# A six-layer decoder on one core: the first layer's "agents" stage with all 32 batches as rows of one PSUM bank

## The reference, cut to what matters

```python
def _L0_attn_ref(x, w_qkv, w_conv1):            # x: (32, 100, 256)
    qkv = jnp.einsum('bnc,dc->bnd', x, w_qkv)
    q, k, v = ...                               # 256 columns each
    agent = jnp.einsum('bnc,c->bn', q, w_conv1)
    agent_attn = softmax(jnp.einsum('bn,bnc->bc', agent * c ** -0.5, k), axis=-1)
    agent_v = softmax(jnp.einsum('bc,bnc->bn', agent_attn, v), axis=-1)
    agent_v = jnp.einsum('bn,bnc->bc', agent_v, v)
    agent_tok = softmax(agent[:, :, None], axis=-1)
    return agent_tok * agent_v[:, None, :]

x = _layernorm(x + _L0_attn_ref(x, ...))
x = _layernorm(x + _L0_xattn_ref(x, ctx, ctx, cell_mask, seq_mask, ...))   # scores + log(cell) + log(seq)
x = _layernorm(x + _L0_ffn_ref(x, ...))         # top 50 of 100 tokens, 16 heads
x = _layernorm(x + _L1_attn_ref(x, ...))        # 16 heads, banded
x = _layernorm(x + _L1_xattn_ref(x, ctx, ctx, ...))
x = _layernorm(x + _L1_ffn_ref(x, ...))         # int8 weights
```

## Time and profile before

| | |
|---|---|
| median of three runs | 1002.06 us |
| the profiled execution | 997.09 us, of which the span from first to last instruction 995.3 us |
| PE busy | 856.5 us, 86% |
| DVE, ACT, POOL busy | 640.5, 510.9, 374.7 us |
| TensorE's mean granted clock | 0.919 of full |
| DMA | 54.11 MB, mean 54 GB/s |
| chain that ended last | PE 56%, DVE 18%, ACT 13%, DMA 4%, POOL 4% |

### The profile page before, as it was taken

One profiled execution on the slowest core, in us unless ns is written; L12 is line 12 of the kernel. 1 busy time (PEld: TensorE's weight loads), 2 busy tenths in 40 slices (PEclk: granted clock), 3 DMA queues, 4 the chain that ended last, 5 costly groups with the idle time before them and its releaser, 6 DMA issues.

```text
span 995.3 us, 19801 instructions
## 1 busy us (share of the span) xinstructions
PE 856.5 (86%) x7054; PEld 642.7 (65%) x7054; DVE 640.5 (64%) x2064; ACT 510.9 (51%) x2392; POOL 374.7 (38%) x528
## 2 busy tenths in 40 slices
PE   7867899989896899997989879899989788989783
PEld 5745777756575777664667758676667666766462
DVE  4224766565878666666687873748665876576546
ACT  3103346887532546864655244776745444666541
POOL 0045502444655132245344430437452542234233
PEclk9766999999798999997999989989979979999697
DMA  7921400001243000012032300003211020000000
GB/s 229 282 62 64 170 1 2 2 17 30 102 159 107 21 10 2 2 40 86 9 102 88 102 18 1 18 8 111 79 33 71 9 97 1 2 2 1 1 9 26
DMA packets 23384, 54.11 MB, mean 54 GB/s; under 512 B 3697, under 2 KB 9589, under 8 KB 23285
## 3 DMA queue, kind: packets, MB, share of 16 engines
q1 hardware_dynamic: 23284, 52.84, 16.3%
HBM read 49.53 MB, written 3.31 MB: 53 GB/s over the span
## 4 chain that ended last, share of the span: by engine, by line
PE 56%; DVE 18%; ACT 13%; DMA 4%; POOL 4%; issue 3%; SPq 1%; DVEq 0%; POOLq 0%; ACTq 0%
PE psum L416 10%; PE psum L421 9%; ACT work L764 7%; PE psum L455 7%; PE psum L441 6%; PE psum L579 4%; PE psum L590 3%; DVE bn L879 2%; ACT work L729 2%; PE psum L600 2%; DVE x L887 2%; PE psum L582 2%; PE psum L411 2%; PE psum L497 1%; PE psum L514 1%
## 5 line engine op out<-in xcount | busy, mean ns | idle before, releaser
L764 ACT ACTIVATE work<-psum,mx 100x100 f32<-100x100 f32 x512 | 169.7, 370 | 52.3 <-DVE mx L1039 52.0
L764 ACT ACTIVATION_READ_ACCUMULATOR work<-psum,mx 100x1 f32 x512 | 119.5, 234 | 0.0
L658 ACT ACTIVATE xT<-psum 128x100 f32<-128x100 f32 (+3 forms) x144 | 52.9, 377 | 112.4 <-PE psum L411 48.1
L1125 POOL TENSOR_SCALAR ve<-mv 100x2 f32<-100x2 f32 x96 | 21.6, 225 | 227.7 <-DVE mv L882 227.2
L455 PE MATMUL psum<-eT,ctx 128*128 128x100 f32 x768 | 97.7, 282 | 0.5 <-DVE eT L916 0.4
L455 PEld LDWEIGHTS psum<-eT,ctx 128*128 128x128 f32 x768 | 94.3, 199 | 2.6 <-issue 0.7
L1154 POOL COPY work<-rden 100x128 f32<-100x128 f32 (+1 forms) x80 | 25.2, 317 | 180.2 <-DVE rden L1043 149.5
L441 PE MATMUL psum<-ctxT,qT 128*100 128x361 f32 x256 | 88.8, 492 | 4.8 <-ACT qT L677 3.9
L658 ACT ACTIVATE eT<-psum 100x400 f32<-100x400 f32 (+3 forms) x128 | 64.3, 517 | 39.5 <-PE psum L618 24.2
L590 PE MATMUL psum<-ident,work 100*100 100x100 f32 x512 | 69.1, 263 | 17.1 <-ACT work L764 16.7
L887 DVE TENSOR_SCALAR x<-res,mv,rstd 100x256 f32<-100x256 f32 x160 | 67.7, 465 | 24.4 <-POOL rstd L1127 24.0
(11 more groups left out here) (228 smaller groups left out, 2005.6 us busy)
## 6 DMA issues: line engine op xcount, KB each, us to landing
ctx<-in_ctx SPq DMA_DIRECT2D x16, 768.0 KB, 7.5
ctxT<-in_ctxT SPq DMA_DIRECT2D x16, 722.0 KB, 5.0
cell<-in_cell SPq DMA_DIRECT2D x16, 282.0 KB
seq<-in_seq SPq DMA_DIRECT2D x16, 282.0 KB
x<-in_x SPq DMA_DIRECT2D x16, 200.0 KB
eT<-agent_rows SPq DMA_DIRECT2D x16, 200.0 KB
out<-xplus SPq DMA_DIRECT2D x16, 200.0 KB
work<-in_x SPq DMA_DIRECT2D x4, 400.0 KB
```

The lines of the kernel that those rows point to most:

```text
L658: return e.activation(dst, src, ACT.Copy, **kw)
L764: last = e.activation(s.e[:, h, :], bk[g][0:S, q * S:(q + 1) * S], ACT.Exp, bias=s.mx[0:S, h:h + 1], accum_out=s.den[0:S, h:h + 1])
```

## The change

The agents' stage keeps its mathematics and changes its form:

- The weights of a batch are now eight columns, of which only the column of its slot is not zero. All 32 batches are accumulated into one bank: batch j of slot i is row 32j + i. DVE writes ag straight into that zeroed room (`token_w` in D's `qT`; `key_w` in A's and B's), and three matmuls with zeros open the banks.
- The first sums are made slot by slot among the transposes. One copy of 256 columns and two transposes take the place of four copies and 16 matmuls, twice. The softmax of the logits is one instruction, its sum is a small matmul, and the division is done on the agent's vector.
- The products of weights change places: `spread` for `wqbk` and the small `bqbk` come behind the logits; `wqk` and `wvo` leave the stage and are made at the start of streams C and D.
- For the first turn a stream does not load its agents from DRAM: two matmuls with a one-hot column spread the rows of `agent_v` (now a tile of its own) over 100 partitions in PSUM, and DVE reads them there.
- The masks of the first turn have rooms of their own in each stream (`v` and `kT`): all four pairs are loaded and multiplied on POOL during the agents' stage; the two DVE instructions, the logarithm and the sum follow in the stream's first turn. `vs` and `v` are cleared there too, stream by stream.
- SP's order: `w8` and `wscale` join `ld_c`; then the four pairs of masks, x, four loads that the second layer needs (`ld_first`), the contexts of A and B, the rest (`ld_const`, now waited for ahead of the pick stage), and the contexts of C and D.
- `ORDER` has new tables for all five engines.

```diff
+        key_w = [s.qT[:, :, :].rearrange("p c t -> p (c t)")[:, 0:SLOTS * B] for s in (SA, SB_)]
...
+        def own_columns(part):
+
+            return bass.AP(tensor=part.tensor, offset=part.offset, ap=[part.ap[0], (ROWS * SLOTS + 1, SLOTS), (SLOTS, ROWS)])
...
-            def rows_to_columns():
+            def weighed(bank, i, weights):
+
+                for j in range(ROWS):
+                    b = ROWS * i + j
+                    last = e.matmul(psum[32 * j:32 * j + SLOTS, bank, 0:D], weights[:, b * SLOTS:(b + 1) * SLOTS], x_of(b),
+                                    start=False, stop=i == SLOTS - 1, skip_group_check=True)
+                return last
+
+            def columns_of_rows():
                 for c in range(NC):
-                    for i in range(SLOTS):
-                        at_ = (c * SLOTS + i) * ROWS
-                        last = e.matmul(psum[:, 7, at_:at_ + ROWS], y_rooms[i // 2][:, i % 2, c * P:(c + 1) * P],
-                                        ident[:, 0:P:32], start=True, stop=True)
+                    last = e.transpose(psum[:, 7, D + c * P:D + (c + 1) * P], yrow[:, c * P:(c + 1) * P], ident[:, :])
                 return last
...
-            for i in range(SLOTS):
-                e.wait_ge(*agent_dve(f"ag{i}"))
-                for j in range(ROWS):
-                    b = ROWS * i + j
-                    last = e.matmul(psum[32 * j:32 * j + 32, i // 2, i % 2 * D:(i % 2 + 1) * D],
-                                    ag[:, b:b + 1].to_broadcast([S, 32]), x_of(b), start=True, stop=True)
-                last.then_inc(*agent_pe.up(f"y{i}"))
-            e.wait_ge(*agent_act("row1"))
-            e.wait_ge(*agent_dve("row1"))
-            rows_to_columns().then_inc(*agent_pe.up("yT1"))
+                if i:
+                    e.wait_ge(*agent_dve(f"ag{i - 1}"))
+                    weighed(7, i - 1, token_w)
+            e.wait_ge(*agent_dve("ag7"))
+            weighed(7, SLOTS - 1, token_w).then_inc(*agent_pe.up("y"))
...
+            e.wait_ge(*agent_act("x15"))
             spread(4, cols["a_bv"], W["a_o"]).then_inc(*agent_pe.up("p0"))
-            spread(5, cols["c_bk"], W["c_qT"]).then_inc(*agent_pe.up("p1"))
+            spread(5, cols["c_bv"], W["c_o"]).then_inc(*agent_pe.up("p2"))
...
-                        last = e.matmul(psum[32 * j:32 * j + 32, i // 4, i % 4 * P:i % 4 * P + S],
-                                        zT[:, c, b:b + 1].to_broadcast([P, 32]), xT_of(c, b),
-                                        start=c == 0, stop=c == NC - 1)
+                        last = e.matmul(psum[32 * j:32 * j + SLOTS, 0, 0:S], key_w[c][:, b * SLOTS:(b + 1) * SLOTS], xT_of(c, b),
+                                        start=False, stop=i == SLOTS - 1 and c == NC - 1, skip_group_check=True)
             last.then_inc(*agent_pe.up("log"))
-            e.wait_ge(*agent_dve("p3"))
+            e.wait_ge(*agent_dve("p0"))
+            spread(4, cols["c_bk"], W["c_qT"]).then_inc(*agent_pe.up("p1"))
+            e.wait_ge(*agent_dve("p2"))
+            for c in range(NC):
+                last = e.matmul(psum[:, 5, 0:1], cols["c_bk"][:, c:c + 1].to_broadcast([P, P]), cols["c_bq"][:, c:c + 1],
+                                start=c == 0, stop=c == NC - 1)
+            last.then_inc(*agent_pe.up("p3"))
+            e.wait_ge(*agent_act("lexp"))
+            e.transpose(psum[0:S, 7, 0:P], lrow, ident[:, :]).then_inc(*agent_pe.up("col"))
+            e.wait_ge(*agent_dve("acol"))
+            for i in range(SLOTS):
+                last = weighed(1, i, token_w)
+            last.then_inc(*agent_pe.up("u"))
+            e.wait_ge(*agent_dve("acol2"))
+            e.matmul(psum[0:B, 6, D:D + 1], acol, ones[0:S, 0:1], start=True, stop=True).then_inc(*agent_pe.up("sum"))
+            e.wait_ge(*agent_dve("p1"))
             for h in range(NC):
...
-                    last = e.matmul(psum[:, 5, h * D:(h + 1) * D], W["c_qT"][:, c, h * P:(h + 1) * P], W["c_kT"][:, c, :],
-                                    start=c == 0, stop=c == NC - 1)
...
-            last.then_inc(*agent_pe.up("p6"))
-            e.wait_ge(*agent_dve("ln"))
-            for i in range(SLOTS):
-                last = e.matmul(psum[0:S, 7, i * ROWS:(i + 1) * ROWS], l_rooms[i // 4][:, i % 4, :], ident[:, 0:P:32],
-                                start=True, stop=True)
...
-                last.then_inc(*agent_pe.up(f"u{i}"))
-            e.wait_ge(*agent_act("row2"))
-            e.wait_ge(*agent_dve("row2"))
-            rows_to_columns().then_inc(*agent_pe.up("yT2"))
+            e.wait_ge(*agent_dve("yr2"))
+            columns_of_rows().then_inc(*agent_pe.up("yT2"))
             e.wait_ge(*agent_dve("yT2"))
             for c in range(NC):
...
+            def weights(w, v):
+                for h in range(NC):
+                    last = columns(bk[1][:, h * D:(h + 1) * D], w, h, lambda c: v[:, c, :])
+                last.then_inc(*s.tensor["start"].up("weights"))
+
             for t in range(TURNS):
+                if t == 0:
+
+                    e.wait_ge(*agent_dve("v"))
+                    if s is SC_:
+                        weights(W["c_qT"], W["c_kT"])
+                    elif s is SD:
+                        weights(W["c_vT"], W["c_o"])
+                    for b in range(NB):
+                        n = NB * s.pair(t) + b
+                        last = e.matmul(bk[0][0:S, b * D:(b + 1) * D], ident[0:B, n:n + 1].to_broadcast([B, S]), agent_v[:, :],
+                                        start=True, stop=True)
+                    last.then_inc(*s.tensor["start"].up("rows"))
+                    yield
                 yield from cross(t, "first", s.vector["mix"], W["x_k"], W["x_o"])
 
...
+            e.memset(token_w, 0.0)
+            for part in key_w:
+                last = e.memset(part, 0.0)
+            last.then_inc(*agent_dve.up("zero"))
...
+                if t == 0 and s in (SC_, SD):
+                    e.wait_ge(*s.tensor["start"]("weights"))
+                    e.tensor_scalar((wqk if s is SC_ else wvo)[:, :, :].rearrange("p c n -> p (c n)"), bk[1],
+                                    INV if s is SC_ else 1.0, None, ALU.mult).then_inc(*s.vector["start"].up("weights"))
                     yield
 
                 pe, act, dve, pool = s.at("mix")
                 e.wait_ge(*s.load_x(t))
-                e.wait_ge(*s.load_agent(t))
+                if t:
+                    e.wait_ge(*s.load_agent(t - 1))
+                else:
+                    e.wait_ge(*s.tensor["start"]("rows"))
                 for b in range(NB):
                     if t:
                         e.wait_ge(*s.vector["quant"](f"x{b}", t - 1))
                     n = NB * s.pair(t) + b
-                    e.scalar_tensor_tensor(s.res[0:S, b, :], s.agent[:, b, :], tok[:, n:n + 1], s.x[0:S, b, :],
-                                           ALU.mult, ALU.add).then_inc(*dve.up(f"r{b}"))
+                    e.scalar_tensor_tensor(s.res[0:S, b, :], s.agent[:, b, :] if t else bk[0][0:S, b * D:(b + 1) * D],
+                                           tok[:, n:n + 1], s.x[0:S, b, :], ALU.mult, ALU.add).then_inc(*dve.up(f"r{b}"))
                 stats(dve, t)
                 yield
...
-
-            e.wait_ge(*agent_pe("u7"))
+            for s in streams:
+                masks_product(e, s, 0)
+
+            e.wait_ge(*SD.gpsimd["mask"]("prod", 0))
+            e.wait_ge(*agent_pe("u"))
             for s in streams:
                 last = e.memset(s.work[32 * (ROWS - 1):P, 0:H * HALF], 0.0)
             last.then_inc(*agent_pool.up("rows"))
-            e.wait_ge(*agent_pool("rows"))
-            e.wait_ge(*agent_dve("w8"))
-            e.wait_ge(*agent_pe("yT2"))
-            for s in streams:
-                e.memset(s.v_pick[:, :, :, :], 0.0)
-                last = e.memset(s.v[:, :, :, :], 0.0)
-            last.then_inc(*agent_pool.up("zeros"))
+            e.wait_ge(ld_first, LD_FIRST)
 
         def gpsimd_turns(e, s):
...
+            def zeros():
+
+                e.wait_ge(*agent_dve("v"))
+                e.wait_ge(*s.gpsimd["mask"]("sum", 0))
+                e.memset(s.v_pick[:, :, :, :], 0.0)
+                e.memset(s.v[:, :, :, :], 0.0).then_inc(*s.gpsimd["start"].up("zeros"))
...
+                if t == 0:
+                    masks_sum(e, s, t)
+                    zeros()
+                    yield
...
-            load_masks(e, SA, 0)
...
-            for n in WEIGHTS:
-                if n not in EARLY and n != "a_o":
-                    weight(n, ld_const)
...
-            e.dma_start(slots[:, :, :], ins["slots"]).then_inc(ld_const, 16)
-            load_ctx(e, SA, 0)
-            load_ctx(e, SB_, 0)
+            e.dma_start(w8_i, ins["w8"].rearrange("(c p) n -> p c n", p=P)).then_inc(ld_c, 16)
+            e.dma_start(wscale[:, :], ins["wscale"].to_broadcast([P, 1])).then_inc(ld_c, 16)
+            for s in streams:
+                load_masks(e, s, 0)
```

(23 more changed lines are left out.)

335 lines of the change are left out of this document (156 added, 179 removed).

## The result

The changed kernel took 1009.15 us (median), the kernel before, beside it on the same chip, 1004.75 us. The ratio is 1.006, with a 95% interval of 1.0039 to 1.0081. The forecast was 982 us.

The account below looks back on a forecast made before the run. PE was taken as the bound, behind a serial agents' stage and a thin ramp. Stage 16.3 plus ramp 4.1, loop nothing, gave 20.4 us off 1002.06: about 982 us, 8 in 10 range 966 to 1000.

Parts of the forecast that it names:

- Link 1: Agents' stage, start of the spread products: at 31.1 instead of 33.77 us, a gain of 2.7 (bounds nothing to 6).
- Links 3 and 5: Agents' stage, logits (4.56 us) and second sums (5.39): nothing gained, within 1 us and minus 2.5 to plus 2.
- Links 2, 4 and 6: Agents' stage, spread products to logits, logits to second sums, sums to vector: gains of 2.7, 5.8 and 5.1 us.
- The ramp: Start of the streams, from the agent's vector to 125 us: 51.4 us instead of 55.5, a gain of 4.1.
- For the loop I take nothing, plus or minus 8 us: Main loop: same instructions, only the order tables new, so no change taken, plus or minus 8 us (1%).
- The slower rival: Loop: streams run too close together and load DVE, 30 us lost against 20 gained, total 1012 us; chance 0.12.
- POOL holding the ramp: Start of the streams: POOL's work delays DVE and streams C and D, ramp gives back 8, 990 us; chance 0.17.
- the end gaining: End of the kernel, 925 to 950 us: three streams fill PE, 9 us come back, 973 or less; chance 0.15.
- The stage that doesn't shorten: Agents' stage: late loads and a lower clock put the vector at 60 us, total 990 to 998; chance 0.08.

Follow-up runs that it names:

- after: The changed kernel itself, with its own new order tables throughout, against the kernel before: 1009.15 us (median), ratio 1.006.
- experiment 3: Changed kernel with its new order only for PE's first 104 steps, the old order for the rest: 986.05 us, ratio 0.9818 to the kernel before.
- experiment 2: Kernel before, with its own order for PE's first 146 steps and the new tables' order for the rest: 1035.99 us, ratio 1.0317.
- the spliced kernel: Same kernel as experiment 3: changed code, new order to PE's step 104, old order behind it: 986.05 us.

## Why the prediction was wrong

- **Link 1** (spread products at 31.1): 30.89, right by luck. I had the last load of `ld_c` decide, and the key product done near 27 or 28. The load had landed at 29.0, and PE went to the spread products straight from the key product, which began at 29.05 and took 1.92, because the first sums ended only at 27.5. (My own terms, 31.85 less 2.2 plus 1.0, also give 30.65 and not 31.1.)
- **Links 3 and 5** (logits and second sums as long as before): too careful. They took 2.8 for 4.56, beyond my bound of 1 us, and 3.5 for 5.39. The granted clock is 1.00 all through to 64 us; before, it was 0.62 in the logits and 0.68 in the second sums, and 4.56 x 0.62 = 2.8, 5.39 x 0.68 = 3.7. I had read durations at a partly lower level as if they were the instructions' own. That is 3.6 us of the 5 by which the vector came earlier than my 53.2.
- **Links 2, 4 and 6** (forecast to last 5.4, 2.6 and 4.2): 5.7, 2.0 and 3.3. Right, to within a microsecond each.
- **The ramp**: a gain of 4.1 forecast. Behind the vector it is 3.7 (25 us of head, 21.3 of them in the stage). D's first transposes came at 74.55, forecast near 75. Right, though the 3 us that I added for a lower clock at its start weren't there (1.00 to 64 us, 0.84 from 64 to 75).
- **"For the loop I take nothing, plus or minus 8 us"** is the step that failed: it put the cost of the new tables at nothing, although the rows could not tell how they fit. The part from 125 us on (100 in after) is 36.5 us longer, and the mark that I had set (PE's share in the loop within 1% of 0.89 at 0.94) came out as 0.85 at 0.91. The order behind the head costs 23 us with one code (experiment 3 against after); in the old code it costs 31 us, seam included (experiment 2). The rest of the 36.5 us is 11 us of PE's busy time, spent on equal instructions, and 3 us of idle time, which the spliced kernel has as well against the profiled execution of before. That execution lay 8 us under the median of its kernel, so this part is partly the spread of the runs; how much isn't settled.
- **The slower rival** had nearly the right time, 1012, and the right place for the worst stretch, an end of turns where three streams run close. It had the wrong price: it let DVE's amount of work starve PE. With 49 us less on DVE the distance to the old order stayed (20.8 us). The mark I had set for it, DVE over 21 and PE under 18 of 25 us, shows once in the loop (775 to 800 us: 22.46 and 17.79); in the worst stretch DVE has only 19.26, for it stands too. What the traces show there is engines that stand in their order at a step that isn't ready, in part for loads that come in one bunch. I gave this rival 0.12. What could have weighed it, each engine's step beside the load or chain that feeds it, I didn't read.
- **POOL holding the ramp** and **the end gaining**: POOL's lock was there (a normalization of 2.59 us at 54.71 and one of 2.64 at 70.90, as 2.12 in the earlier trace rows), but PE had work. The rule of the Trainium skill (SBUF — State Buffer, "Who interferes with whom") that GpSimd and a DVE instruction in a two-port mode lock each other out of a shared pair of ports agrees with these rows. The masks' share of the lock doesn't make the loss in the loop, since cutting them helped the old order as much (1.5%) as the new (1.3%). The end did run better (21.21 us of PE at 0.93 from 925 to 950 us, for 19.51 at 0.59), on top of a loop that had already lost more.
- **The stage that doesn't shorten**: refuted by the first fence.

## What to carry to other kernels

A table of steps is an edit of the whole loop, however small the change beside it: cost it first, by putting the old order into the new code and the new order into the old code, and keep the new one only for the stretch that gains by it. Place the seam with care and try several: seams at steps 60 to 125 lay within 5 us of one another, one at 410 cost 49 us more than the one at 104. To gain from an order, go down the list of the longest waits of the bounding engine, follow each back through the in-order engines to a load, and check on the sync engine's own queue which step it stood at; one swap there was worth 0.5 to 0.8% here, while the swap beside it was worth nothing. Removing a suspect alone (loads, or work) can leave a distance untouched, 22.5 and 20.8 of 23 us here, where removing both left 12.3; take both away before either is acquitted, and run often enough to tell such numbers apart.

## What the runs showed of the hardware

- The logits' 64 matmuls of 100 columns (128 records) took 4.56 us before, at a granted clock of 0.62, the lower level for part of them, and 2.8 us after, at 1.00 throughout: 1.6 times less, as much as the clock gives, though their weights had shrunk from 32 columns to 8. What brought the clock down before isn't shown: from 27.5 us to the logits PE was busy 12.38 of 14.30 us before, and 7.55 of 9.13 after.
- Small DVE instructions between tiles of SBUF were stretched beside POOL's mask products: the scaling of 32x256 elements took 1.58 us from 32.22 and a product of 100x32 elements 1.58 us from 37.51, and each ended within 0.15 us of POOL's product (31.96 + 1.71 and 37.31 + 1.73). Before, the first of them took 0.34 us with POOL idle. A copy out of PSUM beside the next product (34.87, with POOL's from 34.27 to 35.98) kept its 0.23 us.
- Cutting 24 of POOL's operations of 1.7 us to a few columns (36 us less of its busy time, on an engine busy 37% of the span) gave 1.3% of the kernel's time with one order and 1.5% with the other.
